# Expert tiles of a routed feed-forward layer: SwiGLU values kept with features on partitions, a tile's weights copied to a fixed place, 33 tiles of rows gathered ahead

## The reference

```python
logits = jnp.einsum('btc,ec->bte', x, router_w)          # 16 experts
top_vals, top_idx = jax.lax.top_k(logits, 2)
gates = jax.nn.sigmoid(top_vals)
gu = jnp.einsum('nc,ech->neh', xf, gate_up_w)            # 256 -> 2 x 256, each expert
gate, up = jnp.split(gu, 2, axis=-1)
h = jax.nn.silu(gate) * up
out_all = jnp.einsum('neh,ehc->nec', h, down_w)          # 256 -> 256
moe = jnp.einsum('ne,nec->nc', w_full, out_all)          # w_full: the two gates, else 0
shared = jnp.einsum('bts,cs->btc', jax.nn.silu(sg) * su, shared_down_w)
x = x + moe + shared
```

## Time and profile before

| | |
|---|---|
| median of 3 runs | 1411.06 us (1407.27 to 1411.35) |
| profiled execution, first to last instruction (its span) | 1379.5 us |
| difference of the median and the span | 31.6 us |
| PE busy in the span | 1255.7 us (91%) |
| VectorE, ScalarE, GpSimd busy | 888.8, 663.2, 523.9 us |
| expert tiles in the profile | 1222.8 us to the end |

### The profile page before, as it was taken

The page is one execution under the profiler, slowest core; times in us unless marked ns, Lnnn a source line. Parts: engine busy times, 40 slices in busy tenths (PEclk is TensorE's granted clock), DMA queues, the critical chain, the costliest instruction groups (busy, mean ns, idle before and its releaser), DMA issues. The chain is left out here.

```text
span 1379.5 us, 18247 instructions
## 1 busy us (share of the span) xinstructions
PE 1255.7 (91%) x5694; PEld 569.1 (41%) x5694; DVE 888.8 (64%) x2045; ACT 663.2 (48%) x1243; POOL 523.9 (38%) x731
## 2 busy tenths in 40 slices
PE   6898989989999999999999999998899888999996
PEld 3232433323343224453453444443242334666663
DVE  5889789788877986458557567568768423233332
ACT  2355455566555655556546556446656551012221
POOL 4444251163312411326217227225423122456665
PEclk9799999999999999999999999999999999999998
DMA  8472513324330333033123123124622004934341
GB/s 262 131 245 81 159 49 96 109 65 147 110 106 24 108 93 108 22 87 108 47 63 108 47 62 108 47 62 123 139 85 48 17 16 118 337 99 55 55 54 16
DMA packets 113216, 131.53 MB, mean 95 GB/s; under 512 B 17017, under 2 KB 93305, under 8 KB 112867
## 3 DMA queue, kind: packets, MB, share of 16 engines
q1 hardware_dynamic: 102867, 119.91, 30.0%
q0 software_dynamic: 10256, 10.45, 4.6%
HBM read 83.25 MB, written 48.40 MB: 95 GB/s over the span
## 5 line engine op out<-in xcount | busy, mean ns | idle before, releaser
L1288 DVE TENSOR_REDUCE Mx<-bank 128x1 f32<-128x512 f32 x512 | 339.0, 685 | 206.6 <-PE bank L1022 204.5
L904 ACT ACTIVATE prob<-bank 128x512 f32<-128x512 f32 x576 | 332.4, 594 | 257.2 <-PE bank L1048 255.6
L1048 PE MATMUL bank<-QS,KS 99*128 99x512 bf16 x768 | 296.1, 387 | 40.1 <-ACT prob L904 19.5
L1022 PE MATMUL bank<-KS,QS 96*128 96x512 bf16 x768 | 296.9, 388 | 14.2 <-DVE Mx L1285 8.0
L1061 PE MATMUL bank<-prob,V 128*17 128x512 f32 x1536 | 206.6, 610 | 0.7 <-ACT prob L904 0.7
L904 ACT ACTIVATE prob<-prob 128x512 f32<-128x512 f32 x192 | 120.9, 629 | 159.4 <-DVE prob L1299 158.5
L1048 PEld LDWEIGHTS bank<-QS,KS 99*128 99x128 bf16 x768 | 74.8, 98 | 234.2 <-ACT prob L904 130.3
L1022 PEld LDWEIGHTS bank<-KS,QS 96*128 96x128 bf16 x768 | 76.0, 99 | 123.0 <-issue 47.2
L1285 DVE CUSTOM_DVE_ANT_0 bank<-bank,ff_h 128x512 f32<-128x512 f32 x128 | 87.9, 696 | 20.6 <-PE bank L1022 20.0
L741 POOL TENSOR_SCALAR parts<-rest 128x512 bf16<-128x512 f32 x47 | 29.1, 620 | 183.4 <-DVE rest L1248 182.8
L727 POOL TENSOR_SCALAR shift<-mv 128x4 f32<-128x4 f32 x28 | 5.5, 197 | 233.5 <-DVE mv L1209 233.5
(11 more groups left out here) (180 smaller groups left out, 1833.2 us busy)
## 6 DMA issues: line engine op xcount, KB each, us to landing
stack_scr<-parts SPq DMA_DIRECT2D x48, 384.0 KB, 2.6
QS<-stack_scr SPq DMA_DIRECT2D x47, 384.0 KB, 4.1
KS<-stack_scr SPq DMA_DIRECT2D x47, 384.0 KB, 5.0
stack_scr<-parts SPq DMA_DIRECT2D x48, 256.0 KB, 2.9
w_gu<-in_gate_up SPq DMA_DIRECT2D x16, 512.0 KB, 9.6
stack_scr<-parts SPq DMA_DIRECT2D x48, 128.0 KB, 2.9
cT<-in_ctxT SPq DMA_DIRECT2D x8, 512.0 KB, 5.8
w_dn<-in_down SPq DMA_DIRECT2D x16, 256.0 KB, 10.0
```

The costliest lines, as they stand in the source:

```text
L904: act.activation(prob[:, u % NP_, j, :], src, ACT.Exp, scale=CAST).then_inc(exp_done, 1)
L1022: pe.matmul(m, QS[0:STACK, h, qt * P:(qt + 1) * P], KS[0:STACK, h, :], start=True, stop=True).then_inc(s_full, 1)
L1048: pe.matmul(bankT[e % NT][:, :], KS[0:ROWS, h, kt * P:(kt + 1) * P], QS[0:ROWS, h, :], start=not on_pe, stop=True).then_inc(t_full, 1)
L1288: dve.tensor_reduce(dst, b, AX.X, ALU.max).then_inc(s_read, 1)
```

## The change

It does four things in `experts`:

1. The gate-up product swaps its operands: the weights become the stationary operand, in eight blocks of 128 x 128 (4 column blocks times 2 of contraction), and the 128 turned rows stream past. The result has features on partitions and tokens along the bank. The product of Silu and up thus is what the down product needs as stationary operand: `turn_hidden`, the copy to `hTt` and their two semaphores go, and the down product of a tile comes one iteration earlier.
2. The weights of the gate-up product come from a fixed place, `w_now`, with two slots (half 1 of `hid`, free after the shared expert's round 1). ACT reads the tile's expert into a register and copies 128 x 1024 float32 from `w_gu` (`stage`); PE waits for it (`staged`). Two are staged ahead; in its loop ACT does Silu of s, stages s + 2, then `yt` of s - 1.
3. The down product writes to four banks in turn instead of two.
4. NX is 33 instead of 30.

```diff
--- before.py
+++ after.py
@@ -1454,7 +1454,7 @@
         def sem(name):
             return phase.enter_context(nc.semaphore(name))
 
-        NX = 30
+        NX = 33
         ROWS_SEM = 8
         NY = 4
         LATE = B - EARLY_SHARED
@@ -1462,6 +1462,7 @@
         w_dn = sb("w_dn", [P, NE, EH // P, D], F32)
         tile_expert = sb("tile_expert", [1, TILES], I32)
         hid = sb("hid2", [P, 2, HT, S], F32)
+        w_now = hid[:, 1, :, :].rearrange("p (i k) n -> p i k n", i=2)
         iota_t = sb("iota_t", [1, TILES], F32)
         iota_p = sb("iota_p", [P, 1], F32)
         ones_e = sb("ones_e", [P, NE], F32)
@@ -1485,8 +1486,7 @@
         xr = sb("xr", [P, NX, D], F32)
         xT = sb("xT", [P, 3, KD, P], F32)
         sgt = sb("sgt", [P, 2, EH], F32)
-        ht = sb("ht", [P, 2, EH], F32)
-        hTt = sb("hTt", [P, 2, EH // P, P], F32)
+        ht = sb("ht", [P, 2, EH // P, P], F32)
         yt = sb("yt", [P, NY, D], F32)
         bank = [phase.enter_context(nc.psum_tensor(f"ebank{i}", [P, 512], F32)) for i in range(8)]
 
@@ -1506,10 +1506,9 @@
         xT_full = sem("xT_full")
         xT_read = sem("xT_read")
         gu_full = sem("gu_full")
+        staged = sem("staged")
         sg_ready = sem("sg_ready")
         h_ready = sem("h_ready")
-        hT_full = sem("hT_full")
-        hT_read = sem("hT_read")
         yt_full = sem("yt_full")
         yt_read = sem("yt_read")
         sum_out = [sem(f"sum_out{i}") for i in range(NY)]
@@ -1594,18 +1593,31 @@
                     if n >= 2:
                         act.wait_ge(hid_done, n - 1)
                     act.activation(sg[:, n % 2, :], bank[(n % 2) * 2][:, :], ACT.Silu).then_inc(sg_done, 1)
-                for s in range(TILES + 2):
+
+                def stage(s):
+                    e = act.value_load(tile_expert[0:1, s:s + 1], min_val=0, max_val=NE - 1)
+                    act.activation(w_now[:, s % 2, :, :].rearrange("p k n -> p (k n)"),
+                                   w_gu[:, bass.ds(e, 1), :, :].rearrange("p a k n -> p (a k n)"),
+                                   ACT.Identity).then_inc(staged, 1)
+
+                act.wait_ge(w_in, 32 * NE)
+                act.wait_ge(y_full, (LATE - 1) * QT)
+                stage(0)
+                stage(1)
+                for s in range(TILES + 1):
                     if s < TILES:
                         act.wait_ge(gu_full, s + 1)
                         if s >= 2:
                             act.wait_ge(h_ready, s - 1)
                         act.activation(sgt[:, s % 2, :], bank[2 + s % 2][:, 0:EH], ACT.Silu).then_inc(sg_ready, 1)
-                    if s >= 2:
-                        n = s - 2
+                    if s + 2 < TILES:
+                        stage(s + 2)
+                    if s >= 1:
+                        n = s - 1
                         act.wait_ge(yt_full, n + 1)
                         if n >= NY:
                             act.wait_ge(sum_out[n % NY], 16 * (n // NY))
-                        act.activation(yt[:, n % NY, :], bank[6 + n % 2][:, 0:D], ACT.Identity,
+                        act.activation(yt[:, n % NY, :], bank[4 + n % 4][:, 0:D], ACT.Identity,
                                        scale=gate[:, n:n + 1]).then_inc(yt_read, 1)
 
             @block.tensor
@@ -1655,31 +1667,24 @@
                                            identf[:, :])
                     ins.then_inc(xT_full, 1)
 
-                def turn_hidden(s):
-                    pe.wait_ge(h_ready, s + 1)
-                    if s >= 2:
-                        pe.wait_ge(hT_read, s - 1)
-                    for k in range(EH // P):
-                        ins = pe.transpose(bank[4 + s % 2][:, k * P:(k + 1) * P], ht[:, s % 2, k * P:(k + 1) * P],
-                                           identf[:, :])
-                    ins.then_inc(hT_full, 1)
-
-                def gate_up_product(s, e):
+                def gate_up_product(s):
                     pe.wait_ge(xT_read, s + 1)
+                    pe.wait_ge(staged, s + 1)
                     if s >= 2:
                         pe.wait_ge(h_ready, s - 1)
-                    for k in range(KD):
-                        ins = pe.matmul(bank[2 + s % 2][:, :], xT[:, s % 3, k, :],
-                                        w_gu[:, bass.ds(e, 1), k, :].rearrange("p a n -> p (a n)"),
-                                        start=(k == 0), stop=(k == KD - 1))
+                    for m in range(2 * EH // P):
+                        for k in range(KD):
+                            ins = pe.matmul(bank[2 + s % 2][:, m * P:(m + 1) * P],
+                                            w_now[:, s % 2, k, m * P:(m + 1) * P],
+                                            xT[:, s % 3, k, :], start=(k == 0), stop=(k == KD - 1))
                     ins.then_inc(gu_full, 1)
 
                 def down_product(s, e):
-                    pe.wait_ge(hT_read, s + 1)
-                    if s >= 2:
-                        pe.wait_ge(yt_read, s - 1)
+                    pe.wait_ge(h_ready, s + 1)
+                    if s >= 4:
+                        pe.wait_ge(yt_read, s - 3)
                     for k in range(EH // P):
-                        ins = pe.matmul(bank[6 + s % 2][:, 0:D], hTt[:, s % 2, k, :],
+                        ins = pe.matmul(bank[4 + s % 4][:, 0:D], ht[:, s % 2, k, :],
                                         w_dn[:, bass.ds(e, 1), k, :].rearrange("p a n -> p (a n)"),
                                         start=(k == 0), stop=(k == EH // P - 1))
                     ins.then_inc(yt_full, 1)
@@ -1690,18 +1695,16 @@
                 down_products(LATE - 1)
                 pe.wait_ge(w_in, 32 * NE)
                 expert = []
-                for s in range(TILES + 2):
+                for s in range(TILES + 1):
                     if s < TILES:
                         expert.append(pe.value_load(tile_expert[0:1, s:s + 1], min_val=0, max_val=NE - 1))
-                        gate_up_product(s, expert[s])
+                        gate_up_product(s)
                     if s + 2 < TILES:
                         turn_rows(s + 2)
                     if s == 1:
                         pe.wait_ge(y_read, LATE * QT)
-                    if 0 <= s - 1 < TILES:
-                        turn_hidden(s - 1)
-                    if s >= 2:
-                        down_product(s - 2, expert[s - 2])
+                    if s >= 1:
+                        down_product(s - 1, expert[s - 1])
 
             @block.vector
             def _(dve):
@@ -1784,16 +1787,11 @@
                 for s in range(TILES):
                     dve.wait_ge(sg_ready, s + 1)
                     if s >= 2:
-                        dve.wait_ge(hT_full, s - 1)
-                    dve.tensor_tensor(ht[:, s % 2, :], bank[2 + s % 2][:, EH:2 * EH], sgt[:, s % 2, :],
-                                      ALU.mult).then_inc(h_ready, 1)
+                        dve.wait_ge(yt_full, s - 1)
+                    dve.tensor_tensor(ht[:, s % 2, :, :].rearrange("p k n -> p (k n)"), bank[2 + s % 2][:, EH:2 * EH],
+                                      sgt[:, s % 2, :], ALU.mult).then_inc(h_ready, 1)
                     if s + 2 < TILES:
                         read_rows(s + 2)
-                    dve.wait_ge(hT_full, s + 1)
-                    if s >= 2:
-                        dve.wait_ge(yt_full, s - 1)
-                    dve.tensor_copy(hTt[:, s % 2, :, :].rearrange("p k n -> p (k n)"),
-                                    bank[4 + s % 2][:, 0:EH]).then_inc(hT_read, 1)
 
 
 # ---- launch: one core; inputs and outputs as the reference has them ----
```

## The result

The changed kernel takes 1415.09 us (median of 20 runs, 1412.28 to 1420.21) against 1411.07 for the kernel before (20 runs, 1407.27 to 1416.09). The ratio is 1.0033, 95% interval 1.0022 to 1.0044: slower by 4 us where I had forecast 1.8 us less, and just above the range, which ended at 1415.

A forecast was written before the change was run, and what follows sets the result against it. The prediction took the scatter chain to bound the expert stage. An earlier first scatter gave -1.75 us and the other terms 0, so 1411.06 - 1.8 = 1409.3 us, with a range of 1405 to 1415.

The forecast's parts named there:

- What bounds the kernel: Expert stage: after the first scatter, the chain of 47 scatters bounds it, 140.6 us from first to last, not TensorE.
- TensorE's tile: Expert tiles on TensorE: 16 short matmuls take 1.79 us, and a whole tile 2.88 us instead of 3.02.
- rival 1: Gate-up product: short matmuls don't overlap with their weight loads, TensorE becomes the bound, total 1456 or 1476 us; chance 6%.
- ScalarE: Expert tiles on ScalarE: staging copy 1.15 us, a tile 2.10 us, below TensorE's 2.88, so staging adds 0.
- Rival 2: Expert tiles: ScalarE becomes the bound if the staging copy doubles to 2.3 us, total about 1426 us; chance 4%.
- The start of the scatters: Start of the expert stage: the first scatter comes at 1229.6 us, 1.75 us earlier than before.
- The gathers between scatters: Scatter chain on POOL: three gathers moved ahead give nothing, since the next scatters wait for landings; uncovered, 3.9 us.
- rival 4: Scatter chain: the three moved gathers do pay, or landings get shorter, total 1405.4 us; chance 12%.
- The gathers ahead: Before the first scatter: three more gathers at 1.25 us each end at 1228.4, early enough to cost nothing.
- The base of the sum: Whole kernel: the runs' median lies 31.6 us above the profiled span, and stays so around the new span.
- The sum: Whole kernel: earlier first scatter -1.75 us, gathers 0, TensorE's shorter tile 0, staging 0; 1.8 us less in all.
- Rival 3: Expert tiles: TensorE idles more and its clock falls to 1.2 GHz; ten such tiles cost some 20 us; chance 2%.

The follow-up runs named there:

- after_nostage: Changed kernel with 30 gathers ahead and no staging copy, every tile reading expert 0's weights from their place: 1409.88 us, ratio 0.9986 to the kernel before.
- before_again: The kernel before, unchanged, profiled once more: span 1409.0 us, the execution's own time 1410.77 us.
- before_late: The kernel before with 4 gathers ahead, the other 26 held until the shared expert's last hidden values are written: 1408.49 us, ratio 0.999.

## Why the prediction was wrong

- **What bounds the kernel.** After S0 the scatter chain does, and its sum held nearly: 140.5 and 141.2 us in the new profiles against 140.6. TensorE's 91% was no guide. Right, but for the 0.7 us of the longer landing wait, which the prediction put at nothing.
- **TensorE's tile.** The chain shows 16 short matmuls in 1.78 to 1.79, for 1.79 forecast:

```profile
1258.25 1.78 PE ebank L1677 x16
1260.04 0.22 PE ebank L1666 x2
1260.25 1.79 PE ebank L1677 x16
```

  This answers to the earlier trace rows: a load takes 0.192 us on average in this profile and the entries still come each 0.112, so that loads and short matmuls overlap with real weights and rows too, and rival 1 is out. The rule of the Trainium skill ("TensorE: Matmul & The Clock Gate", Part 3, "What overlaps and what doesn't") doesn't hold for this stream of full 128 x 128 blocks.
- **ScalarE.** The staging copy took 1.057, for 1.15 forecast from the earlier trace rows:

```profile
L1599 ACT ACTIVATE hid<-w_gu x47: 1040/1057/1059, 1250.6 to 1396.5; 128x1024 f32 x47
```

  Hidden, as `after_nostage` shows. Rival 2 is out.
- **The start of the scatters.** S0 comes 7.0 us after the first gate-up product, for 6.8 forecast (1229.6 less 1222.8), and 8.7 before. The gain is 1.76, for 1.75 forecast. Right.
- **The gathers between scatters.** The three that left cost nothing there: the gaps S28 to S29, S30 to S31 and S32 to S33 keep 4.60, 4.46 and 4.25. Right, and rival 4 is out.
- **The gathers ahead: the step that failed.** The prediction has them end at 1228.4, before anything needs them, and puts them at nothing. Their cover was judged by POOL's own time alone. In the timed executions a series of gathers issued one right behind the other keeps VectorE and ScalarE from acting on TensorE's results; three more lengthen TensorE's idle time from 21.3 to 24.5 us, and undoing them brings it back to 21.2 and gives the loss back. "TensorE starts tile 0 at 1222.79 as before" failed with it.
- **The base of the sum.** The 31.6 us between the span and the median were taken as lying around the span. 29.5 of them lay inside: 23.0 are the hole, and 6.7 lie ahead of the gathers. Of some 90 timed runs of the kernel before none is below 1404.8 us, so that the execution of the earlier trace rows was the exception. Why it had neither delay stays open; it had the same gathers at the same pace. The base of the forecast, 1411, was right all the same, since it was the median itself; what the wrong place hid was the hole that more gathers lengthen.
- **The sum, done again.** By the table: -1.8 for the earlier S0, +3.5 for the gathers ahead instead of nothing, +0.7 for the landing wait, +0.3 at the end: 2.7 us more. The runs say 4.0 to 4.7. The 1.3 to 2 us between are of the size by which the first gather comes later, the table's first row.

Shown are: that the hole goes with the gathers' number and place, not with their bytes or landing waits, and, by one run, that 0.8 us more between two of them removes it ahead of the tiles. What exactly is late, TensorE's completion signals or the writes behind its recorded starts, isn't shown; that VectorE and ScalarE are late in the same stretch only argues for the signals. One rival is untested: every timed run here was recorded too, with its span and clock, and no run shows whether the hole is there without recording. The 1.6 or so by which the first gather seems to start later in kernels with the new code isn't told apart from the spread of executions. Rival 3, a falling clock, didn't come between the tiles; the clock fell in the hole.

## What to carry to other kernels

A span far below the median of the timed runs is a warning that the profile shows another execution than those timed: take it again before building a sum on it. Here gathers issued back to back by GpSimd were not free to the other engines, though POOL had the time and nothing waited for their data. In a kernel of this kind issue few ahead, put the others into waits that are there anyway, and look at the engines on the other side while they are issued. Whether an engine has "time left" for a piece of work depends on what that work does to the others too, and an experiment that moves it shows this.

## What the runs showed of the hardware

- With 30 indirect gathers issued each 1.25 us, results of TensorE were acted on up to 25 us late and TensorE stood still for 21 us. With 16 they were up to 9 us late and TensorE's wait was 1.7 us; with 30 each 2.08 us apart there was none before the tiles. The lateness began 7 to 12 us after the first of a series (12 in `before_again`, 7 in `before_late`, 9 behind the eight DMAs from 1107 us on). Narrowing each row from 1024 to 64 bytes changed nothing.
- Float32 matmuls of 128 columns, each with its own 128 x 128 weights, come each 0.112 us, loads included, over 16 in a row, at a granted clock of 1.00.
- Two gathers of 1.31 us fit unseen into the 4.5 to 4.7 us between two scatters that wait for each other's landing.
